# Attention kernel: the value products of two score steps issued as one block, at every second step

## The reference

```python
# layer 0: group norm, attention over channels (32 x 32 per head), projection, residual
# layer 1: one attention head over the 1024 pixels, 32 channels for q and k, 128 for v
s = jnp.einsum('bcn,bcm->bnm', query, key_);  attn = softmax(s, axis=2)
y = jnp.einsum('bcm,bnm->bcn', value, attn);  o = einsum('oi,bihw->bohw', Wo, y) * gamma + x
# layers 2 and 3: group norm, qkv, 8 heads of 32 channels, attention over the 1024 pixels
sim = jnp.einsum('bhdi,bhdj->bhij', q, k);    attn = softmax(sim, axis=-1)
out = jnp.einsum('bhij,bhdj->bhid', attn, v)  # then a projection with bias, and a residual
```

## Time and profile before

| | |
|---|---|
| time, median of 3 runs | 3344.45 us (3338.95 to 3347.55) |
| profiled execution | 3339.21 us, its span 3337.3 us |
| busy share of the span | PE 87%, POOL 70%, DVE 56%, ACT 47% |
| mean granted TensorE clock | 0.926 of full speed |
| chain that ended last | PE 54%, POOL 14%, issue 13%, DMA 6%, DVE 5%, ACT 5% |
| six steady turns | about 567 to 2807 us |

### The profile page before, as it was taken

The page is one execution under the profiler, slowest core; times in us unless marked ns, Lnnn a source line. Parts: engine busy times, 40 slices in busy tenths (PEclk is TensorE's granted clock), DMA queues, the critical chain, the costliest instruction groups (busy, mean ns, idle before and its releaser), DMA issues.

```text
span 3337.3 us, 46964 instructions
## 1 busy us (share of the span) xinstructions
PE 2901.6 (87%) x12840; PEld 1431.4 (43%) x12840; DVE 1853.0 (56%) x3293; ACT 1553.8 (47%) x2794; POOL 2336.4 (70%) x781
## 2 busy tenths in 40 slices
PE   5678868999989998999989998999989999886686
PEld 3334334454445444554435444554445444432332
DVE  0255227556665666566664666566665667662461
ACT  1225323545554455545554455545554455553153
POOL 2228524868886787778876787778886788988087
PEclk8779877999999999999999999999999999998698
DMA  1150033331441334332440334332440334330320
GB/s 57 28 71 27 11 51 53 53 49 29 52 84 19 40 53 66 53 49 39 52 80 13 40 53 66 53 49 39 52 81 12 40 52 65 41 40 1 57 34 14
DMA packets 74159, 151.71 MB, mean 45 GB/s; under 512 B 9073, under 2 KB 10609, under 8 KB 73906
## 3 DMA queue, kind: packets, MB, share of 16 engines
q1 hardware_dynamic: 73906, 148.56, 28.9%
HBM read 20.46 MB, written 16.78 MB: 11 GB/s over the span
## 4 chain that ended last, share of the span: by engine, by line
PE 54%; POOL 14%; issue 13%; DMA 6%; DVE 5%; ACT 5%; SPq 1%; POOLq 0%; ACTq 0%; DVEq 0%
POOL acc L756 13%; PE psum L1210 12%; PE psum L1232 9%; PE psum L1181 9%; PE psum L1132 4%; PE psum L1156 4%; PE psum L1140 3%; DVE maxpart L972 3%; PE psum L1228 3%; DMA Q<-lo 3%; DMA K<-hi 3%; ACT prob L853 2%; PE psum L1253 2%; PE psum L1074 2%; ACT ha L780 1%
## 5 line engine op out<-in xcount | busy, mean ns | idle before, releaser
L756 POOL TENSOR_TENSOR acc<-acc,prob 128x2048 f32<-128x2048 f32 (+1 forms) x480 | 1870.0, 3896 | 202.9 <-ACT prob L853 171.6
L972 DVE TENSOR_REDUCE maxpart<-psum 128x1 f32<-128x512 f32 x2176 | 1404.1, 683 | 881.7 <-PE psum L1181 853.0
L853 ACT ACTIVATE prob<-psum 128x512 f32<-128x512 f32 x2176 | 1224.2, 596 | 1040.0 <-PE psum L1210 1003.8
L1210 PE MATMUL psum<-Q,K 104*128 104x512 f32 x2048 | 1080.8, 530 | 112.1 <-ACT prob L853 58.7
L1181 PE MATMUL psum<-K,Q 96*128 96x512 f32 x2048 | 860.4, 430 | 61.8 <-DMA K<-hi 49.6
L1210 PEld LDWEIGHTS psum<-Q,K 104*128 104x128 f32 x2048 | 396.0, 194 | 817.9 <-ACT prob L853 423.1
L756 POOL TENSOR_TENSOR acc<-prob 128x2048 f32<-128x2048 f32 (+1 forms) x80 | 312.2, 3903 | 601.7 <-ACT prob L853 316.3
L1232 PE MATMUL psum<-prob,vT 128*32 128x512 f32 x4096 | 581.7, 628 | 0.0
L1181 PEld LDWEIGHTS psum<-K,Q 96*128 96x128 f32 x2048 | 413.3, 202 | 216.7 <-issue 83.9
L1232 PEld LDWEIGHTS psum<-prob,vT 128*32 128x32 f32 x4096 | 102.2, 111 | 209.1 <-ACT prob L853 115.9
L1253 PE MATMUL psum<-acc,ones 128*32 128x512 f32 x640 | 93.6, 659 | 84.8 <-POOL acc L756 84.8
(11 more groups left out here) (110 smaller groups left out, 1969.6 us busy)
## 6 DMA issues: line engine op xcount, KB each, us to landing
Q<-hi SPq DMA_DIRECT2D x128, 256.0 KB
K<-hi SPq DMA_DIRECT2D x128, 256.0 KB
Q<-lo SPq DMA_DIRECT2D x64, 256.0 KB
K<-lo SPq DMA_DIRECT2D x64, 256.0 KB
xa<-in_x SPq DMA_DIRECT2D x8, 1024.0 KB, 8.4
scratch<-xa SPq DMA_DIRECT2D x8, 1024.0 KB, 4.1
xb<-scratch SPq DMA_DIRECT2D x8, 1024.0 KB, 4.9
out<-hb SPq DMA_DIRECT2D x8, 1024.0 KB, 5.4
```

Of the source, the lines that this page charges most:

```text
L756: pool.tensor_tensor(total, first if a == 1 else total, this, ALU.add).then_inc(added, 1)
L853: act.activation(prob[STEP_STARTS.slot(b, start)][:, j, :], score_bank[(SCORES.rank[b.n][e] - 1) % SCORE_BANKS], ACT.Exp, scale=1.0 if lay ...
L972: dve.tensor_reduce(maxpart[layer][:, a // NQ, a % NQ:a % NQ + 1], bank, AX_X, ALU.max).then_inc(max_free, 1)
L1210: pe.matmul(score_bank[(r - 1) % SCORE_BANKS], left, right, start=True, stop=True).then_inc(score_full, 1)
```

## The change

Value blocks are issued only at the end of an even step: then the four products of each of two steps go out together, eight in a row. A step stays behind after it, as before. In an odd step PE issues scores, maxima and side pieces alone. Finish, invert and scale move from 4, 6 and 9 slots after the group's last value block to 8, 10 and 13, so the finish stands at the end of step 2 of the next group in place of step 1. The output pieces that read the scaled result start at slot 19 (16 before), and the pieces of layer 1's output and of layer 2's norm inside (3, 1) move by 1 to 4 slots. Where a part ends with layer 1, the sums that are still due are flushed ahead of the last group's value products. Lines of the changed kernel are 3 higher from `plans()` on (`L1232` is `L1235`).

```diff
-FINISH_AFTER = 4
-INVERT_AFTER = 6
-SCALE_AFTER = 9
-SCALED = 16
+FINISH_AFTER = 8
+INVERT_AFTER = 10
+SCALE_AFTER = 13
+SCALED = 19
...
-                 (3, 1, at((12, 13, 14, 15, 16), out1[:T * NQ + 1])
-                  + at((17, 17, 18, 18, 19, 21, 24, 28, 29, 30, 31), out1[T * NQ + 1:]),
+                 (3, 1, at((16, 17, 18, 19, 20), out1[:T * NQ + 1])
+                  + at((20, 20, 21, 21, 22, 24, 27, 29, 30, 31, 31), out1[T * NQ + 1:]),
...
                 while late:
+                    if late[0][0] == "value" and late[0][3:] == (0, 0):
+                        plan += [x for _, x in pending]
+                        pending.clear()
                     advance(plan)
...
-                while j == HPT - 1 and len(late) > LAG:
+                while s % 2 == 0 and j == HPT - 1 and len(late) > LAG:
                     advance(plan)
```

## The result

The changed kernel takes 3517.8 us (median of 4 runs, 3511.9 to 3522.8) where the kernel before takes 3341.7 us beside it (3331.8 to 3347.6): ratio 1.053, 95% interval 1.050 to 1.056. The prediction was 3315 us, with 3288 to 3347 as its range.

What follows compares the result with a forecast made beforehand. PE was taken to set the pace in steady turns, POOL's chain in closing parts. Steady turns -28, other parts -8.6 and +7.0 give -29.6: 3339.2 becomes 3309.6 us, 3315 as the runs' median; range 3288 to 3347.

Steps and rivals of the forecast that it cites:

- The price of a block: Two value blocks together take 1.86 us to the next score; one takes 1.00; a pair saves 0.27 us, at most 0.33.
- The pair without side pieces: Two steps without side pieces, where ACT paces the scores: 6.47 us in place of 6.66, 0.19 us saved.
- the one on the moved sums: Later finish, addition, scale and piece in steady turns: shift together, with the traded waits all within one step.
- -2.3 us in (3, 1): Loss per turn: output piece's wait 1.10 to 1.6 us, moments' wait 2.01 to 2.9, last step's lost cover 0.9.
- -1.6 +1.1 us in (2, 2): Per turn: second side piece behind the finish waits 1.6 us for its bank; the finish's 1.16 us wait for POOL goes.
- The 4.7 us a turn: Net saving per steady turn: 8.6 - 1.1 - 1.6 - 2.3 + 1.1; 28 us in six turns.
- rival 2: Blocks were cover: in odd steps with side pieces ACT or DVE paces; no change, 3345 to 3353 us; chance 0.17.
- Rival 3: The moments' wait, 2.0 then 2.9 us, drops the clock; about 3 us per turn lost, 3333 us; chance 0.10.
- -8.6 and +7.0 us: Other parts: 32 PE-paced pairs save 0.27 us each; three end-of-part drains lose 2.0, 2.0 and 3.0 us.
- POOL as the bound (1): POOL's later additions bound the steady turns: slower, 3363 us if POOL is 8 us later; chance 0.13.
- The end of (2, 0) (4): Forecast: 7.81 us wait there stays; rival: a later store removes it, up to 33.6 us less, 3281 us; chance 0.08.
- a granted clock below 0.96 in the steady turns: Sign that the forecast is wrong through a clock drop after the moments' wait; the clock was 0.97 before.

Runs made afterwards that it cites:

- the spare products: Changed kernel with three unneeded 128x512 products ahead of each of four PE waits a turn: 3476.5 us, ratio 1.040; same in the kernel before: 3370.2 us, 1.009.
- the third and the fourth kernel: Layer 1 not bunched: changed kernel, also with sums of (3, 0) and (1, 0) at old slots, 3467.8 us; kernel before with bunching only, old sums, 3366.6 us.
- Two accumulators alone: Changed kernel with two accumulators used in turn for POOL's sums, layer 3 running with layer 2's weights: 3512.9 us, ratio 1.052.
- the control: Kernel before with two accumulators (layer 3 on layer 2's weights) and the scaling moved from POOL to DVE: 3408.9 us, ratio 1.022.

## Why the prediction was wrong

**The price of a block: right.** 1.86 us were predicted and 1.85 measured. 32 pairs by 0.27 = 8.6 us a turn was the first term; "rest" fell by 7.6 us in the changed kernel, or by 6.1 with idle time at half clock counted once: 71 to 88% of it. The pair without side pieces was wrong: at the end of (3, 0), from block to block, two steps took 6.63 us before and take 6.60 now, where 6.66 and 6.47 were forecast. Next to nothing is saved where there are no side pieces.

**The step that failed** is the one on the moved sums. It let "all of finish, addition, scale and piece move together", priced the move at -2.3 us in (3, 1) and -1.6 +1.1 us in (2, 2), and closed with "The waits that this trades against one another are all within one step." Late sums alone cost 18.1 us a turn: 10.2 us of idle time and 8.6 us of clock; there output pieces that wait for POOL's scaling are 44.7 of the 61 us by which PE's waits grew in six turns, and a single such wait is up to 5.7 us, longer than a step. The 4.7 us a turn that the prediction had as saved came out as 23.8 lost. In the changed kernel the terms themselves were near. The out piece waits for 1.99 us (predicted 1.6), the moments for 2.17 (2.9), the piece in (2, 2) for 1.48 (1.6). Two things were missing.

The first is DVE's inversion. It stood in slot 9 of the next group, in the step that a value block ends; now it stands in slot 13, in the step that has no block. The timeline of the changed kernel in (2, 1), 7 rows of PE and DVE:

```profile
1394.28 0.71 DVE L999 STREAM_TRANSPOSE turned_sums<-psum 128x512 f32<-128x512 f32 x1
...
1394.42 0.50 PE L1184 MATMUL psum<-K,Q 96*128 96x512 f32 x1
1394.76 0.40 PE L1213 MATMUL psum<-Q,K 104*128 104x512 f32 x1
1395.03 0.25 DVE L1002 RECIPROCAL inverse<-turned_sums 128x16 f32<-128x16 f32 x1
...
1395.31 0.71 DVE L1003 STREAM_TRANSPOSE turned_sums<-inverse 128x512 f32<-128x512 f32 x1
...
1395.95 0.65 DVE L975 TENSOR_REDUCE maxpart<-psum 128x1 f32<-128x512 f32 x1
...
1396.65 0.80 PE L1184 MATMUL psum<-K,Q 96*128 96x512 f32 x1 [1.49 <-DVE maxpart L975]
```

For 1.67 us DVE does the inversion and frees none of the three banks; PE, with nothing but scores and maxima to issue, is through them and waits for 1.49 us, and 6.8 us at half clock follow. This is rival 2 in kind ("the blocks were cover"), at another place than it named, and its sign came true: the waits for ACT and DVE grew by 8.4 us a turn. With late sums and no bunching the waits for DVE are 18.7 us in the six turns, with bunching and the old sums 12.9, with both in layers 2 and 3 35.3, in the changed kernel 46.1. That the inversion is what DVE is late by was read from the timeline; no run put it back behind a block.

The second is the clock. Rival 3 had the mechanism, tied to one wait and priced at 3 us a turn with a chance of 0.10. It is 20.8 us a turn, the largest term of the loss: "half" went from 12.2 to 33.0. The prediction weighed each wait by its length; the spare products show that what follows it has to be added. The Trainium skill (TensorE: Matmul & The Clock Gate, Part 1) has the half clock follow an idle window, which had been cited. The trace agrees only in part: 10 of the 13 drops of the third turn follow waits of only 0.7 to 2.2 us, with products close ahead and behind. The question of the clock should have been asked of each new wait in the sum.

**What bunching does to a turn.** On the old sums it takes 6.4 us of "rest" away, and gives 5.2 of idle time and 3.2 of clock back. On the late sums, in layers 2 and 3 alone, it takes 6.7 us of "rest" and 0.9 of idle time away and gives 8.8 of clock back. Layer 1's bunching and the late sums of (3, 0) and (1, 0) add 4.4 us a turn.

**Layer 1 and the other parts: wrong in sign.** The sum had -8.6 and +7.0 us outside the steady turns. The four other parts are 9.6, 12.5, 9.6 and 4.1 us longer between the first exponential of each and that of the next (the last: to the end); the stretch ahead of the first exponential is 5.8 us shorter. In the first two, most of it lies in one place. POOL and PE in the first part of the changed kernel:

```profile
125.40 7.13 PE L1231 MATMUL psum<-prob,products 128*128 128x512 f32 x16
...
127.43 1.26 POOL L737 TENSOR_TENSOR att<-att,turned_sums 128x512 f32<-128x512 f32 x1 [13.66 <-DVE turned_sums L1003]
...
128.65 1.26 POOL L759 TENSOR_TENSOR acc<-prob 128x512 f32<-128x512 f32 x1
...
130.05 8.28 POOL L759 TENSOR_TENSOR acc<-acc,prob 128x512 f32<-128x512 f32 x6
...
138.48 1.93 PE L1256 MATMUL psum<-acc,ones 128*32 128x512 f32 x8 [5.95 <-POOL acc L759]
```

The seven additions of (1, 1) stand behind the finish and the scaling of (1, 0), and this finish now comes 12.2 us after (1, 1)'s first exponential, where it came after 7.2. They end 26.2 us after the group's first exponential, where they ended after 18.1, and (1, 1) with its gap is 8.8 and 8.3 us longer. Layer 1's bunching is the cause, with late sums or without: with bunching alone the stretch is 10.2 and 8.8 us longer than before, with layer 1 left out of it, in the third and the fourth kernel, within 1.2 us of before. Two accumulators alone leave it at 107.1 and 107.6 us; with the scaling taken off POOL too it is 5.1 and 5.4 us longer than in the control. In the earlier trace rows such a wait was seen in the closing parts alone.

**The rivals.** POOL as the bound (1): not shown. The finish waits of the steady turns are gone, and freeing POOL's queue did not bring their time back; it may hold a part, and in the first two parts it does. The blocks as cover (2) and the clock (3): both came true, together and larger. The end of (2, 0) (4): unchanged, as forecast. The test "a granted clock below 0.96 in the steady turns" is the one that told: 0.92.

**Open.** Half clock also lies at the end of (2, 2), for 13.7 us in the changed kernel and 6.8 before, with no idle time over 0.3 us within 8 us ahead of it. With spare products it is two stretches of 3.4 us there, with no such product near; no run here explains it. Why (3, 0) and (2, 0) lose 4.2 and 2.9 us each was read from the trace alone: the scores that follow the q and k pieces wait 1.75 us for ACT, which waits for a stacking DMA, in a step that had a block before.

## What to carry to other kernels

When work is taken from one place of the busiest engine's stream, ask which short job of the other engines it used to cover, and where that job stands once other events are renumbered; here an inversion of 1.67 us stood where a block was due, and no wait for DVE was over 0.6 us; where none was due, 1.49 us of waiting and 6.8 us at half clock followed one. Price a new wait of TensorE at its length plus half of the half-clock stretch behind it, read from a wait of like length in the trace, and look at how busy PE is ahead of it. Before moving an operation to another engine, look at how long it lasts there while the first engine is at work. And split a change that moves two things before judging either: here a late finish in three groups wins 0.5%, nearly everywhere it loses 2.2%. Set the parts beside a kernel that has just their edits: 3.5 and 0.5% are less than the changed kernel's 5.3%, but 3.5 and 0.8% are not less than the 3.7% of the kernel that joins those two.

## What the runs showed that was not expected

Waits of 0.7 to 2.2 us were enough to be followed by 3.4 to 6.8 us at half clock, in the changed kernel in 46 of 55 cases above 1.4 us and 9 of 22 below. In the turn of the earlier trace rows of the kernel before, waits of 1.10 and 2.01 us in the same place of (3, 1) were followed by none. Spare products, in such waits or ahead of one, made a kernel faster by 41 us. And an operation of 0.7 us moved from POOL's queue to DVE's cost 2.6%: it took 2.3 us in the mean, as it ended only 0.55 us after the addition that POOL was at when it started.
